# Norms of a two-layer transformer turned by DMA instead of TensorE, modulation as token rows, new plans

## What is computed

```python
# layer 0
n = x * rsqrt(mean(x*x) + EPS);  h = n * (w * (1.0 + t @ tw.T))[:, None, :]
# layer 1
h = _ln(x) * (scale + 1.0) + shift       # scale, shift, gamma from silu(cond) @ Wada.T + bada
x = x + attn(h1) * gamma1;  x = x + mlp(h2) * gamma2
```

## Time and profile before

| | |
|---|---|
| median of 3 runs | 2541.29 us |
| the profiled execution, first to last instruction | 2537.9 us |
| TensorE busy | 2479.0 us, 98% |
| VectorE, GpSimd, ScalarE busy | 55%, 42%, 36% |
| TensorE clock granted, mean | 0.989 of full speed |
| DMA queue of SyncE | 149.15 MB, 20.9% of 16 engines |

### The profile page before, as it was taken

The page is one execution under the profiler, slowest core; times in us unless marked ns, Lnnn a source line. Parts: engine busy times, 40 slices in busy tenths (PEclk is TensorE's granted clock), DMA queues, the critical chain, the costliest instruction groups (busy, mean ns, idle before and its releaser), DMA issues.

```text
span 2537.9 us, 47183 instructions
## 1 busy us (share of the span) xinstructions
PE 2479.0 (98%) x18438; PEld 1230.8 (48%) x18438; DVE 1392.1 (55%) x2118; ACT 918.1 (36%) x1496; POOL 1064.3 (42%) x1007
## 2 busy tenths in 40 slices
PE   6799999999999999999999999999999999999999
PEld 5344444444444444444454445554545455554544
DVE  7564342443434434344586575766757585775752
ACT  4342221222212222132343452626445262634532
POOL 3333232332322222232354464656556465655632
PEclk7899999999999999999999999999999999999999
DMA  7631112111121111211322312021221202111110
GB/s 226 200 98 32 53 22 60 25 36 49 21 64 21 41 45 21 64 21 46 126 78 88 116 31 80 26 68 40 55 60 31 81 26 74 45 52 52 33 60 29
DMA packets 188885, 152.08 MB, mean 60 GB/s; under 512 B 120463, under 2 KB 131855, under 8 KB 188693
## 3 DMA queue, kind: packets, MB, share of 16 engines
q1 hardware_dynamic: 188692, 149.15, 20.9%
HBM read 75.83 MB, written 18.74 MB: 37 GB/s over the span
## 4 chain that ended last, share of the span: by engine, by line
PE 86%; DVE 4%; POOL 4%; issue 3%; ACT 2%; DMA 1%; SPq 1%; POOLq 0%; DVEq 0%; ACTq 0%
PE ps_m L1590 48%; PE ps_abef L1590 19%; PE ps_d L1590 3%; PE ps_c L1590 2%; PE ps_abef L1775 2%; PE ps_abef L1782 2%; PE ps_abef L1777 2%; PE ps_abef L1811 1%; PE ps_d L1761 1%; PE ps_c L1644 1%; PE ps_abef L1819 1%; POOL inner L947 1%; PE ps_abef L1800 1%; POOL scratch L975 1%; PE ps_d L1663 1%
## 5 line engine op out<-in xcount | busy, mean ns | idle before, releaser
L1590 PE MATMUL ps_m<-h_mlp,weights 128*128 128x512 f16 x3168 | 722.8, 380 | 9.1 <-issue 3.7
L1590 PE MATMUL ps_m<-weights,inner 128*128 128x512 f16 x3072 | 693.9, 379 | 2.1 <-DVE scratch L1423 2.1
L947 POOL TENSOR_TENSOR inner<-scratch,inner 128x512 f16<-128x512 f32 x256 | 314.3, 1228 | 438.6 <-ACT inner L1124 438.5
L1590 PEld LDWEIGHTS ps_m<-h_mlp,weights 128*128 128x128 f16 x3168 | 304.6, 98 | 362.6 <-issue 14.6
L1590 PEld LDWEIGHTS ps_m<-weights,inner 128*128 128x128 f16 x3072 | 296.7, 98 | 336.4 <-issue 4.0
L1590 PE MATMUL ps_abef<-h_mlp,weights 128*128 128x512 f16 x1440 | 328.9, 379 | 0.0
L1124 ACT CAST inner<-scratch 128x512 f16<-128x512 f32 x256 | 156.7, 612 | 180.3 <-DVE scratch L1423 108.6
L1590 PEld LDWEIGHTS ps_abef<-h_mlp,weights 128*128 128x128 f16 x1440 | 137.9, 98 | 163.5 <-issue 2.8
L987 POOL TENSOR_TENSOR scratch<-scratch 128x512 f32<-128x512 f32 x64 | 72.6, 1134 | 158.1 <-DVE scratch L1477 158.1
L925 POOL TENSOR_TENSOR h_attn<-scratch,h_attn 128x512 f16<-128x512 f32 x64 | 77.2, 1206 | 122.6 <-ACT h_attn L1087 122.6
L1087 ACT CAST h_mlp<-scratch 128x512 f16<-128x512 f32 x64 | 39.5, 617 | 238.9 <-POOL scratch L987 142.2
(11 more groups left out here) (164 smaller groups left out, 3472.6 us busy)
## 6 DMA issues: line engine op xcount, KB each, us to landing
x_mlp<-x_attn SPq DMA_DIRECT2D x64, 256.0 KB, 2.6
scratch<-scratch SPq DMA_DIRECT2D x128, 128.0 KB
weights<-gamma SPq DMA_DIRECT2D x128, 128.0 KB, 3.0
x_attn<-x SPq DMA_DIRECT2D x32, 256.0 KB, 2.7
x_mid<-x_mlp SPq DMA_DIRECT2D x32, 256.0 KB, 2.0
x_attn<-x_mid SPq DMA_DIRECT2D x32, 256.0 KB, 2.6
out<-x_mlp SPq DMA_DIRECT2D x32, 256.0 KB, 2.2
inner<-wada_t SPq DMA_DIRECT2D x4, 1024.0 KB, 6.7
```

What stands on the lines that cost most here:

```text
L947: nc.gpsimd.tensor_tensor(inner[:, 1, j, :], src, inner[:, 0, j, :], ALU.subtract).then_inc(L.m_lo, 1)
L1590: ins = nc.tensor.matmul(o, left(a, k), right(b, k), start=(first and n == 0), stop=(last and n == len(order) - 1), skip_group_check=True)
```

## The change

- **Norms after block 0 of layer 0.** `turn_x` and the PSUM `gain` are gone for 56 norms of layer 0 and all 64 of layer 1. The modulated norm is made in token rows: in layer 0 one VectorE step (x times `rstd` times gain row), in layer 1 two (x minus mean, times gain; times `rstd`, plus shift). ScalarE and GpSimd cut it into `turned`, one buffer of 128x1024 float16 (high and low side by side), and a DMA transpose (`flip`) writes it feature-major into `h_attn` or `h_mlp`. The GpSimd `shift` step of layer 1 is gone. The 8 norms of layer 0's block 0 stay on TensorE.
- **Rows of modulation.** Before each norm two DMAs (`fetch`) spread the gain row (layer 1: gain and shift, 1024 float32) of each of the tile's two sequences over 64 partitions. All eight tables are multiplied in row form; two more small products (`g0`, `g1`, 8 columns wide, 32 instructions each by the same form as line 1614) give block 0 of layer 0 its feature-major gains.
- **A tile ahead.** The first norm of the next block's tile 0 (`tile 4`) is made at the end of the running block, so `proj` of tile 0 no longer starts from that block's own plan.
- **Banks.** Layer 0's `out` goes to `ps_c` instead of `ps_abef`; in layer 1 `ps_d` is `out`'s alone. The gated output is written over `gamma_a`.
- **Waits.** `proj` and the first MLP product wait for `flip` instead of `h_hi` and `h_lo`. One semaphore per tile replaces the counts of hand-overs and stores. `hand` and `next` are plan stages of their own.
- **Plans.** The generators are replaced by tables with a written time for every stage and every MLP step of four matmul groups; all five plans have a new order. The last steady block of each layer is written out after the loop.

```diff
-    nc.vector.tensor_scalar(xn, xa[:, t, :], moments[:, 0:1], rstd, ALU.subtract, ALU.mult).then_inc(L1.xn, 1)
...
-    nc.vector.tensor_tensor(by_seq(h32), by_seq(ps_d), gain("norm" + stage[4], t), ALU.mult).then_inc(L1.h_scaled, 1)
+    dve.wait_ge(L1.stat, m + 1)
+    dve.wait_ge(L1.tables, 32 * (m + 1))
+    dve.wait_ge(L1.h_lo, m)
+    nc.vector.scalar_tensor_tensor(xn, xa[:, t % TILES, :], moments[:, 0:1], gain_row, ALU.subtract, ALU.mult).then_inc(L1.xn, 1)
+    dve.wait_ge(L1.rstd, m + 1)
+    dve.wait_ge(L1.xn, m + 1)
+    nc.vector.scalar_tensor_tensor(xn, xn, rstd, shift_row, ALU.mult, ALU.add).then_inc(L1.h32, 1)
...
+def norm_hi(L, src, it, kind, t):
...
+    act.wait_ge(L.h32, n + 1)
...
+        act.wait_ge(L1.flip, 16 * n)
+    nc.scalar.copy(turned[:, 0], src).then_inc(L.h_hi, 1)
...
+def turn_norm(L, kind, t):
+    dst = h_attn[:, t % TILES % 2] if kind == "norm1" else h_mlp[:, :, :, t * P:(t + 1) * P]
+    sp.dma_start(dst.rearrange("p a k n -> p (a k) n"), turned.rearrange("p a n -> p (a n)"),
+                 transpose=True).then_inc(L.flip, 16)
...
+def fetch1(it, kind, t):
...
+    sp.wait_ge(L1.h32, *counts(norm_no(L, it, kind, t)))
+    for b in range(2):
+        row = seq_rows(mod1_dram[int(kind[4]) - 1].rearrange("s k d -> s (k d)"), *block_of(it, t), b)
+        dst = rows_t[SEQ * b:SEQ * (b + 1)].rearrange("p k n -> p (k n)")
+        sp.dma_start(dst, row.to_broadcast([SEQ, 2 * D])).then_inc(L1.tables, 16)
...
+def flip1(it, kind, t):
...
+    sp.wait_ge(L1.h_lo, cut_done)
...
+        sp.wait_ge(L1.up, free)
+    turn_norm(L1, kind, t)
...
-                if stage in ("turn_x1", "turn_x2"):
-                    pe.wait_ge(L1.xn, norm_no(norms, it, "norm" + stage[6], t) + 1)
-                    d_free(plan, at, it)
-                    for c in range(KC):
-                        ins = nc.tensor.transpose(ps_d[:, P * c:P * (c + 1)], xn[:, P * c:P * (c + 1)], ident32[:])
-                    ins.then_inc(L1.nt, 1)
...
-                                pe.wait_ge(L1.h_lo, (it + 1) * 2 * TILES)
+                                pe.wait_ge(L1.flip, 16 * norms_until(L1, it))
...
-            with pe.Fori(1, NBLK - 1) as i:
+            with pe.Fori(1, NBLK - 2) as i:
                 block1(i, True)
+            block1(NBLK - 2, True)
```

968 lines of the change are left out of this document (598 added, 370 removed), and 75 rows, old and new, of tables (LAST1_AT, SETUP_START0, SETUP_START1, SETUP_TRANS).

## The result

The changed kernel takes **2560.6 us** (median of 4, 2554.55 to 2564.5) against 2540.98 for the kernel before (median of 4): 1.0075 times as long, 95% interval 1.006 to 1.009. The forecast was 2487, with 2508 as its upper end, and a chance of 0.04 for slower.

What follows compares the result with a forecast made beforehand. TensorE, busy 2479.0 of 2537.9 us, was taken as the bound. The terms -54.7 + 3.5 + 0 + 1.4 - 4 = -53.8 gave 2484.1 us profiled, 2487 at the median; range 2466 to 2508, to hold 8 in 10.

Steps and rivals of the forecast that it cites:

- Step 1: Both layers' norms: 120 sets of transposes leave TensorE at 0.44 us each, with short bank waits also gone: -54.7 us.
- The rule against it: Skill page advice to turn 128x128 blocks on TensorE: 390 ns there against 1309 ns by DMA; eight blocks an estimated 10.5 us.
- Step 2: End of a layer 1 block: norm chain 10.3 us against 11.6 of cover; 0.5 us each, +3.5, ends 0 and +31.
- Step 3: End of a layer 0 block: the same chain under the 41 us down product, slack 4.8 us, cost 0.
- Step 4: Other engines in steady stretches: none bound with 58% to 64%, SyncE and DMA have room, cost 0.
- Step 5: Set-up and FIRST0: table work -3 to +5 us, 0 on the path; +1.4 at its end, -4 for order at start and entry.
- B: Block boundaries of both layers: the transpose lands late, slower than before; 2567 us at a landing of 8 us; chance 0.04.
- C: Landings of 4.5 to 6 us in layer 1, or mid-block waits: +8 to +28, 2495 to 2515 us; chance 0.16.
- D: TensorE's work falls but waits of another engine that bounds refill its time: 2541 us; chance 0.02.

Runs made afterwards that it cites:

- e15: The changed kernel with TensorE's loop over layer 1's blocks 1 to 5 written out as straight code; 2540.3 us, ratio 0.9998.
- e18: The changed kernel with e7's three cuts in layer 1's norms and TensorE's layer 1 loop written out; 2508.72 us, ratio 0.9881.
- e7: The changed kernel with layer 1's GpSimd low half and second VectorE norm step on 32 of 512 columns, later row fetches 64 values a row; 2522.16 us.
- e10: The changed kernel with the set-up's first two row-table products using one of four chunks of the conditioning vector; 2544.21 us, ratio 1.0019.
- e2: The changed kernel with GpSimd's low-half subtraction in layer 1's norms cut to 32 of 512 columns; 2541.25 us, ratio 1.0013.
- e4: The changed kernel with the 64 row fetches after layer 1's first block bringing 64 values a row instead of 1024; 2548.76 us, ratio 1.0032.

## Why the prediction was wrong, step by step

**Step 1 was right.** 143.0 us of TensorE work is left in a block of layer 1, where 146.5 - 8 x 0.44 makes 143.0; a block of layer 0 is 3.8 us shorter (3.5 forecast). In layer 0 this came through in full, 26.8 us. The price by starts, 0.44 us a set, held. TensorE's busy time as a whole fell by 29.2 and not 53 because 25.8 us came off in the seven blocks of layer 0 and only 12.9 in those of layer 1, some of which ran partly at the lower clock, and 9.5 were added at the start (8.5) and between the layers.

**The rule against it.** The price of a 128x128 block by DMA in the Trainium skill, page "VectorE: DVE Perf Modes", section "The three transpose paths", taken eight times, would have meant landings of an estimated 10.5 us. The trace disagrees: the flips land in 3.1 at the median, with their issue of 1.24 us. In layer 1 the norm's steps on SBUF told more than the transpose itself.

**Step 2 was right in place, and mis-sized.** I gave the chain from the end of `out` 10.3 us against a cover of 11.6. In the block from 1708.69 on, `out.3` ends about 137.1 us in; the second step of the norm starts at 141.7 and takes 1.75 us instead of 0.75 (it lies beside the output step on GpSimd); `hi` ends at 144.2, `lo` at 145.4; the flip is issued at 145.5 and lands 5.2 us later: 13.6 us in place of 10.3, 2 over the cover. Both terms that were read from undisturbed rows, 0.73 for the step and 3.1 for the landing, were too low in just this place. The landing was late at the heads behind the jump, with TensorE's instruction packet beside it; the rows in front, which the prediction had named, make 0.4 us. The sign of error that I had named, a wait of over 1 us in each block, stands at four heads of seven. It was inside my bound of +31 for seven boundaries, and the trace of before had the landing in its worst case. What I had no term for is the gap of 1.1 to 1.6 us behind the jump, and the lower clock in some blocks (about 1.6 us for each place). By e15 and e18 all of this is 2.1 to 2.5 us a block, by the spread above perhaps half of it.

**Step 3 was right.** Layer 0 shows no wait at its turns (159.90 of 160).

**Step 4 was the step that failed.** "None is bound with 58% to 64%" priced the norm's SBUF work at nothing. Those shares are means over a stretch with two unlike halves. In the up half VectorE had up to 93% of some 10-us windows before, which I could have read and didn't; it has 91% over 50 us now. And a step with two SBUF operands did not keep its price when GpSimd was given another such step beside it: `arg` went from 732 ns to 1008, 818 without GpSimd's low half, and VectorE's busy time from 97.8 us a block to 105.2. The added work is 3.6 to 4.0 us a block (e7, e18; 2.7 against e10), some 28 us over the seven periods of layer 1. What is left with all three parts gone, 1.3 to 1.5 us a block, is a wait at `mix`; its cause stays open, and no reordered plan was tried without the added work.

**Step 5 was wrong in sign.** I had the six changed tables at -3.3 and `g0` and `g1` at up to +8.1, and none of it on the path, "in a stretch with 37.8 idle". The eight row tables cost 4.1 us each where 3.55 was forecast, the small products 11.5 where 8.1 was the upper end. And idle time in a stretch does not mean that work put there is free: TensorE's queue is in order, and this work stands ahead of the second tile's transposes. The first product came at 129.00, 9 us from 120, where more than 8 was named as a sign of error. At the entry to layer 1, for which I had -4 together with the start, TensorE has six waits of 0.7 us or more, 9.6 us in all, where before it had two with 2.9, and it is busy 1.0 us longer although the transposes are gone, at a mean clock of 0.98; the stretch takes 7.8 us longer. e2 and e7 give back 3.0 and 4.3 of that, so part of it is the same crowding. The rest was not settled.

**Rivals.** B foresaw slower by a late landing in both layers; layer 0 shows none, and in layer 1 the last flip lands late at four heads of seven, at up to 5.2 us, where B's formula gives 2 x 5.2 - 8.6 = 1.8 us a boundary: about the wait that stands there, though the formula counts two late landings, and far from eating 54.7 us. C had the right kind, "waits in the middle of a block where the new order leaves less than 1 us", but its price of at most 28 us on the sum is what the added work alone cost. D, to which I gave 0.02, is the nearest: TensorE's work fell, and its time was refilled. Its stated objection, no engine above 65% in steady stretches, is step 4 again.

**Where the difference lies.** From the 2484.1 us forecast for the profiled execution to the span of 2552.8 it is 68.7 us. The seven blocks of layer 1 hold 46 of it (+25.1 measured; steps 1 and 2 make it 7 x (-3.5 + 0.5) = -21). The other 23 lie at the start and between the layers, where some 25 more were lost and layer 0 gave 2 back.

## What to carry to other kernels

Price a step that moves to a side engine in the busiest 10-us windows around its place, not by the engine's mean share, and take an SBUF step with two operands at the price it has beside another engine's such step. Putting latency in the place of work was free here where a whole norm's chain, fetch to landing, was covered: in layer 0 under a 41 us down product, and not in layer 1 under 11.6 us. Before moving stages by hand, take the suspected work out once: one such run showed more than four reordered plans. And keep a run that leaves the suspected part alone: e10 moved the median by 16 us without touching layer 1, as much as a single cut in it.

## What was unexpected of the hardware

- At the head of a block that TensorE reached by a loop jump, a 16 KB instruction packet fell beside the last DMA transpose, which landed in 4.6 to 5.2 us instead of 3.5. Five matmuls on, TensorE stopped for 1.13 to 1.56 us until 1.3 to 1.4 us after a second such packet; with 512 KB of rows in transfer the stop was 3.06 to 3.29. It is not tied to a wait at the jump: e4 has a stop of 1.54 at a head with no wait, and e10 has the waits and no stop. With five turns of TensorE's loop written out the median fell by 20 us.
- A wait of 1.72 and one of 1.52 us close together, and in the same block one of 2.64 us at `mix`, were each followed by a stretch at the lower clock level, and the block's matmuls took 146.3 us instead of 143.1. The block before it had 1.18, 1.56 and 2.64 and stayed at 1.00.
- A float32 step on VectorE with two SBUF operands, 0.73 us alone, took up to 2.61 beside GpSimd steps of the same kind.
